# Layer 1 of a two-layer transformer kernel: dispatch tables built in the stage before, keys turned instead of projected twice

## The reference, cut to what matters

```
xn = layernorm(x)                          # 2048 tokens of 256
q, k, v = silu(xn @ Wq), silu(xn @ Wk), silu(xn @ Wv)     # 16 heads of 16
# linear attention in chunks of 128 tokens, per head with decay ld:
scores = (q k^T) * D ;  o = scores v + (q S) * q_decay
S = chunk_decay * S + (k * k_decay)^T v
attn = rmsnorm_per_head(o * sigmoid(xn @ Wg1 @ Wg2)) * norm_w @ Wo
# mixture of experts: 8 experts, 2 for each token, hidden width 512
rw, sel = top_k(softmax(xn @ w_router), 2) ;  rw = rw / sum(rw)
ffn = sum over the 2 chosen e of rw_e * (silu(xn @ w_gate[e]) * (xn @ w_up[e])) @ w_down[e]
out = x + attn + ffn
```

## Time and profile before

| | us |
|---|---|
| median of 3 runs | 1018.13 |
| lowest and highest | 1017.15, 1026.66 |
| the profiled execution's own time | 1027.36 |
| its span, first to last instruction | 1025.4 |
| PE busy in the span | 863.5 (84%) |
| DVE busy | 576.3 (56%) |
| ACT busy | 407.2 (40%) |
| POOL busy | 312.3 (30%) |
| data moved by DMA | 130.52 MB, mean 127 GB/s |

### The profile page before, as it was taken

How to read it: one execution, slowest core, us unless ns; L and a number is a source line. 1 busy time by engine, 2 the same in 40 slices (tenths; PEclk the granted TensorE clock), 3 DMA queues, 4 the chain that set the end, 5 groups by cost and what they waited for, 6 DMA issues and landing times. The chain is left out here.

```text
span 1025.4 us, 14999 instructions
## 1 busy us (share of the span) xinstructions
PE 863.5 (84%) x4608; PEld 501.9 (49%) x4608; DVE 576.3 (56%) x1269; ACT 407.2 (40%) x686; POOL 312.3 (30%) x250
## 2 busy tenths in 40 slices
...
GB/s 270 127 58 143 200 196 186 117 212 54 104 72 55 125 110 127 73 108 109 135 81 75 93 33 156 224 264 271 148 91 104 103 115 94 88 93 89 73 174 143
DMA packets 158625, 130.52 MB, mean 127 GB/s; under 512 B 64144, under 2 KB 140192, under 8 KB 158560
## 3 DMA queue, kind: packets, MB, share of 16 engines
...
...
## 5 line engine op out<-in xcount | busy, mean ns | idle before, releaser
L1291 DVE TENSOR_REDUCE b_negmax<-b_psM 128x1 f32<-128x512 f32 x256 | 162.9, 683 | 59.0 <-PE b_psM L1453 56.3
L1222 ACT ACTIVATE b_probs<-b_psE 128x512 f32<-128x512 f32 x256 | 138.9, 594 | 117.2 <-PE b_psE L1471 116.4
L1453 PE MATMUL b_psM<-b_kst,b_qst 96*128 96x512 bf16 x256 | 99.1, 429 | 34.3 <-DVE b_negmax L1291 17.7
L1471 PE MATMUL b_psE<-b_qst,b_kst 98*128 98x512 bf16 x256 | 89.1, 409 | 15.2 <-ACT b_probs L1222 11.1
...
L1990 PE MATMUL d_psG<-d_w,d_xT 128*128 x156 | 76.8, 615 | 3.0 <-issue 2.1
L1480 PE MATMUL b_psV<-b_probs,b_vst 128*32 128x512 f32 x512 | 74.8, 658 | 2.8 <-ACT b_probs L1222 2.8
L1822 POOL TENSOR_TENSOR d_rs<-d_ss,d_neghalf 128x16 f32<-128x16 f32 x16 | 47.0, 2938 | 98.9 <-DVE d_ss L1918 98.9
L1998 PE MATMUL d_psU<-d_w,d_xT 128*128 x156 | 74.9, 603 | 0.0
L2015 PE MATMUL d_psY<-d_w,d_hidden 128*128 x312 | 74.8, 382 | 0.0
L1471 PEld LDWEIGHTS b_psE<-b_qst,b_kst 98*128 98x128 bf16 x256 | 20.6, 98 | 106.0 <-ACT b_probs L1222 52.1
L1453 PEld LDWEIGHTS b_psM<-b_kst,b_qst 96*128 96x128 bf16 x256 | 24.2, 99 | 94.2 <-DVE b_negmax L1291 68.1
...
...
## 6 DMA issues: line engine op xcount, KB each, us to landing
...
```

What stands on the lines that cost most here:

```text
L1222: nc.scalar.activation(probs[k % PSLOTS][:, h, :], psE[h % 2][:, :], ACT.Exp, scale=float(HD) ** -0.5).then_inc(scores_used[h % 2], 1)
L1291: nc.vector.tensor_reduce(negmax[i][:, t, h:h + 1], psM[:, h % 2, :], AX_X, ALU.max, negate=True).then_inc(rows_used[h % 2], 1)
L1453: nc.tensor.matmul(psM[:, h % 2, :], qst[g][0:STACK, h, t * P:(t + 1) * P], kst[g][0:STACK, h, :], start=True, stop=True).then_inc(rows_re ...
L1471: nc.tensor.matmul(psE[h % 2][:, :], kst[g][0:STACKM, h, k * P:(k + 1) * P], qst[g][0:STACKM, h, :], start=True, stop=True).then_inc(score ...
```

## The change

1. **Tables move.** `Dispatch` is now built in `middle`. `take`, `put` and `expert` outlive the stage. In the steps of batch 3, DVE gets `prepare` after slot 9, `pick` and `positions` after slot 12, `spread_ids` (inblk, ids) after 13, `spread_rows` (inrow) after 14, `owners` and `tables` after 15; PE gets `rank` after slot 12 and `invert` after 15. The three constants are loaded at the start of `middle`, ahead of the loads of head groups 2 and 3.
2. **Gathers first.** `layer1_main` begins with the four gathers on POOL, and SP loads ident, the weights of expert 0 and then chunk 0. The place of `weights_loaded` is as before. In `main_order` the steps of chunk 0 are no longer in front: all 16 chunks are dealt between the blocks from block 1 on. `outputs` moves from step 6 to step 5, right behind `updates`.
3. **Keys turned.** The second projection of the keys goes, with its silu on ACT. Instead PE transposes the k that slot 12 has made (`turn_k`, 8 transposes, slot 13), and DVE's `decay_k` reads them from PSUM in slot 13. The gate moves from slot 13 to 14 and waits there for `kd_done` (not alone). Wk is loaded once.

```
-            loop(sp, attend, {SLOTS - 8: (store_xn,), SLOTS - 4: (store_q,), SLOTS - 3: (store_gate,), SLOTS - 1: (store,)})
+            loop(sp, attend, {SLOTS - 8: (store_xn,), SLOTS - 4: (store_q,), SLOTS - 2: (store_gate,), SLOTS - 1: (store,)})
...
-                               12: (silu_half(1),), 13: (gate,), 14: (silu_kk,),
-                               15: (silu_v,)})
+                               12: (silu_half(1),), 14: (gate,), 15: (silu_v,)})
...
             def decay_k(n):
-                dve.wait_ge(kk_done, n + 1)
+                dve.wait_ge(k_ps, n + 1)
+                dve.wait_ge(stored, STORES * n)
...
-                               7: (normalise, find_next), 8: (split_xT,), 10: (copy_low, fold_next(0)), 11: (copy_lowT, fold_next(1)),
-                               12: (route_weights, fold_next(2)), 13: (first_part, fold_next(3)), 14: (second_part,),
-                               15: (third_part, decay_k)}, ready)
+                               7: (normalise, find_next), 8: (split_xT,), 9: (prepare,), 10: (copy_low, fold_next(0)), 11: (copy_lowT, fold_next(1)),
+                               12: (route_weights, fold_next(2), place), 13: (first_part, decay_k, fold_next(3), spread_ids),
+                               14: (second_part, spread_rows), 15: (third_part, finish_tables)}, ready)
...
+            def turn_k(n):
+                pe.wait_ge(half_done, 2 * n + 2)
+                for t in range(TILES):
+                    for k in range(KT):
+                        at = t % 2 * D + k * P
+                        mm = nc.tensor.transpose(psX[:, t // 2, at:at + P], half[:, k, t * P:(t + 1) * P], ident[:, :])
+                mm.then_inc(k_ps, 1)
...
-                              8: (turn_x,), 9: (project_half(0),), 10: (logits_low,), 11: (turn_low,), 12: (project_half(1),),
-                              13: (project_gate,), 14: (project_tokens(0, gate_done, kk_ps),),
-                              15: (project_tokens(1, kk_done, v_ps),)}, ready)
+                              8: (turn_x,), 9: (project_half(0),), 10: (logits_low,), 11: (turn_low,), 12: (project_half(1), rank),
+                              13: (turn_k,), 14: (project_gate,), 15: (project_v, invert)}, ready)
...
-    order = [("rank", 0, 0)]
-    order += [("light", *step) for step in steps[:7]]
-    order.append(("invert", 0, 0))
-    order += [("light", *step) for step in steps[7:first]]
-    rest = steps[first:]
-    order += [("turn", 0, 0), ("turn", 1, 0), ("gate", 0, 0), ("up", 0, 0), ("turn", 2, 0)]
-    slots, used, given = BLOCKS * 5, 0, 0
+    order = [("turn", 0, 0), ("turn", 1, 0), ("gate", 0, 0), ("up", 0, 0), ("turn", 2, 0)]
+    slots, used, given = (BLOCKS - 1) * 5, 0, 0
...
-            dispatch.load(sp, io)
+            sp.dma_start(ident[:, :], io["ident"]).then_inc(ident_in, 16)
+            load_weights(0)
             load_chunk(0)
...
-            load_weights(0)
             load_weights(1)
             load_chunk(1)
             for e in range(2, E, 2):
                 load_weights(e)
                 load_weights(e + 1)
                 weights_loaded(e - 2)
                 weights_loaded(e - 1)
                 load_chunk(e // 2 + 1)
...
                 elif s == 5:
                     updates(n)
-                elif s == 6:
                     outputs(n)
```

157 lines of the change are left out of this document (85 added, 72 removed).

## The result

The changed kernel is slower by 0.74%: in 20 runs each, beside one another, the median is 1028.37 us (1022.68 to 1034.75) against 1022.85 us (1016.13 to 1032.89), and the ratio is 1.0074 with a 95% interval of 1.005 to 1.0098 (the quotient of the two medians alone is 1.0054, so differences of 0.2% between ratios say little). A second measurement gave 1.0081 (1.0048 to 1.0114). I had forecast a ratio of 0.998 and a time of 1016 us in a range of 1006 to 1027 us. The profiled execution of the changed kernel took 1029.67 us, its span is 1027.9 us.

What follows compares the result with a forecast made beforehand. PE bounds the expert stretch; engine-to-engine chains bound the two stretches ahead. Terms -7.7 + 5.0 + 5.3 + 0 - 3.5 - 1.1 = -2.0 us, from the median 1018.13 to 1016 us, range 1006 to 1027.

Steps and rivals of the forecast that it cites:

- Part 1: Start of the last stage: first gate 30.7 us after the barrier instead of 38.4, -7.7 us (-13.2 to -5.6).
- third rival: Last stage: `load_chunk(2)`, held behind chunk 0, releases experts 2 and 3 late; some 1040 us; chance 0.05.
- Part 2: Expert stretch: chunk 0's 66 matmul records now fall where PE is busy, +5.0 us (0 to +7).
- hand-offs are a little tighter: Expert stretch: steps stand at 0.92 of the places between expert matmuls, not 0.83; no size of its own.
- Part 3: End of `middle`, batch 3 alone: v's store goes out behind k's third part, +5.3 us (+4 to +6.5).
- v starts at about the same time as before, since it needs the gate's PSUM: End of `middle`, batch 3 alone: v is ready at about 631 to 632 us as before.
- The block by POOL: Batch 3 alone: POOL's subtraction holds DVE's inblk, two SBUF operands, adding 0.9 us; `decay_k`, one PSUM operand, is not blocked.
- Part 4: Attention with steps beside it: looped batches 0 us (-3 to +5 for both), last batch -3.5 us (-5 to -1).
- the gate waits for kd: Looped batches: POOL delays `decay_k`, +6 us for two; gain beside the last batch goes to 0; 1026 us; chance 0.12.
- Part 5: Start of `middle`: POOL's second weight subtraction halves, so its masking of the decay ends earlier, -1.1 us (-1.5 to +1).
- that gap: Whole kernel: profiled execution of 1027.36 us lies 0.9% above the median of 1018.13 us, claimed not to affect the sum.
- the signs by which I wanted to see myself wrong: First gate under 26 us, v's store early, looped slots 13 to 15 over 1 us shorter, or less expert-stretch PE idle.

Runs made afterwards that it cites:

- e_ready: Changed kernel, but SP releases expert 0 right behind the four constants, ahead of the later weights and chunk 1; ratio to before 0.9865.
- e_out6: Changed kernel with `outputs` back at step 6, as before the change; ratio to before 1.009.
- e_front: Changed kernel with chunk 0's twelve steps ahead of the first gate and chunks 1 to 15 dealt from block 0 on; ratio to before 1.0006.
- e_gate5: Changed kernel with DVE's `gate_out` and POOL's power of a chunk at step 5 instead of 6; ratio to before 0.9963.
- e_keys: Kernel before with part 3 of the change alone (keys turned, gate in slot 14 behind kd, Wk loaded once); ratio to before 1.0005.
- e_same: Kernel before, unchanged, profiled a second time; ratio to before 0.9979, profiled execution 1025.48 us.
- e_order: Changed kernel with the gate back in slot 13, transposes in 14, `decay_k` in 14 and `second_part` in 15 of looped batches; ratio to before 1.0047.
- e_late: Changed kernel with `first_part` of k in slot 14 and `second_part` in 15 unless the batch is alone; ratio to before 1.0055.
- e_after2: Changed kernel, unchanged, measured and profiled a second time; ratio to before 1.0081, span 1050.6 us.
- e_same3: Kernel before, unchanged, profiled beside the changed one for the second comparison; span 1035.3 us.
- e_same2: Kernel before, unchanged, profiled a third time, on the chip of the second set; span 1039.2 us.
- e_before_late: Kernel before with `first_part` of k moved to slot 14 and `second_part` to 15 (not alone), nothing else; ratio to before 1.0073.

## Why the prediction was wrong, step by step

**Part 1, the start of the last stage: right.** -7.7 us forecast, -7.7 and -7.8 measured; 30.2 us behind the barrier for 30.7, with 49 DMAs in 30 us and the second chunk's first six in 6.07 us for 7.16. (Of the 7.6 us that I put down to those six, only 4.1 are theirs, 7.16 less six at 0.51; the rest lay in the six behind them and in weight DMAs. The total was right all the same.) PE idled 21.2 us at half clock, ended by SP. e_ready shows that this release, and no data, was late. My third rival, a later release held by chunk 0, did not come: PE waits for SP ahead of the first gate and of no other.

**Part 2, chunk 0 in the expert stretch: the mechanism right, the term mis-sized.** +5.0 (0 to +7) forecast, +9.4 and +13.8 measured, above my upper end. The busy time was well counted (6.2 us for 5.7). What failed is the step "hand-offs are a little tighter", which carried no number. "Moving `outputs` next to `updates` costs nothing" held, for e_out6, which undoes the move, is no shorter (324.9 us); but it missed what the move made possible. I had set the idle time to zero because PE had 9.1 us of it to spare. But that idle was itself hand-offs of a chunk's steps; another chunk and closer steps add to it (+3.7 us) and do not fill it. e_front shows that the cost is that of chunk 0 among the blocks (with the closer steps that it brings; the two were not tried apart), and e_gate5 shows the chain: heads, `gate_out`, POOL's power, d_normed.

**Part 3, the end of the middle stage: about right, by a chain that was half wrong.** +5.3 forecast, +5.5 and +6.7 measured; v's store at 633.95 is where I had it once the 4.6 us of the parts ahead are taken off (638.1 - 4.6 = 633.5). The step "v starts at about the same time as before, since it needs the gate's PSUM" failed: the old gate ran ahead of k's silu, the new one behind the transposes and at half clock (3.78 us), and v came 4 to 7 us later. In the changed kernel it is hidden behind the third part of k, with 2.5 us to spare, so that the number held by luck; but it is why part 3 alone gains nothing at this end (e_keys, +3.7 to e_same and +1.8 to the first profile, against my -2). The base had its share too: in the profile that I read the 48 matmuls of keys and v took 8.7 us, in the three others of that kernel 6.0 at full clock, and the barrier stood 33.8 to 34.0 us behind the split and not 35.9.

The block by POOL came as priced. inblk, with two operands in SBUF, took 2.50 us beside POOL's subtraction (621.45 to 623.57) and ended 1.35 us behind it, where the same operation took 1.49 us in the earlier trace rows without POOL; `decay_k`, one operand in PSUM, took its 1.22 us beside the same POOL instruction, unblocked. There `decay_k` had begun 0.16 us ahead of POOL; in the second looped batch of e_order POOL was first, and it was not blocked either:

```profile
480.09 2.12 POOL L1207 TENSOR_TENSOR b_half<-b_half,b_part 128x1024 f32<-128x1024 f32 x1 [15.43 <-PE b_psX L1639]
481.69 1.21 DVE L1402 TENSOR_TENSOR b_kd<-b_psX,b_kdec 128x1024 f32<-128x1024 f32 x1
```

By the Trainium skill (SBUF — State Buffer, "SBUF: two separate sides"), which has the shared pair of ports as an exclusive lock against DVE operations with two SBUF inputs, this is what has to come; the trace agrees, and shows for `decay_k` what no row of before could.

**Part 4, looped batches: wrong.** 0 (-3 to +5) forecast, +3.9 and +2.3 measured, and +6.1 in the slots concerned. The step that failed: "Taking ACT's silu and two table loads and 16 of 24 PE instructions from slots 13 and 14 therefore lets ACT and PE arrive earlier at the same DVE". They do arrive earlier, but the gate then waits for kd, which is queued behind that very wait of DVE. This is my rival "the gate waits for kd", and its price (3 us a batch) is what the slots show, for another reason than the one it named: not POOL's lock on `decay_k`, which is not blocked, but `first_part` ahead of it. The rival's other half, that the gain beside the last batch goes, did not come in the first set (-5.0 us, more than my -3.5) and did in the second (-0.6). e_order and e_late each take this loss out of the slots, by the place of the gate and by the place of `first_part`. The ratio fell with them by 0.34% and 0.26%, less than the 9 us of the slots, so how much of the whole loss this is stays open.

**Part 5:** -1.1 forecast; slots 0 and 1 of the first batch, from 235.5 to 249.1 us before, are 2.6 us shorter (1.0 and 2.3 in e_after2 against e_same3 and e_same2), about what was forecast or more. The whole stretch ahead of the first split is 2.8 and 0.9 us shorter.

**The base.** "nothing in the sum depends on that gap, so I take it from the median": that median was of three runs, and 20 gave 1022.85. Of the 12.4 us between 1016 and 1028.37, 4.7 are this; moved up by them, my range would have been 1011 to 1032 us and held the result, but the direction would have been as wrong as it is. The rest is parts 2 and 4: chunk 0 and the looped batches cost 8.3 and 11.1 us more than forecast in the two sets; in the first, the last batch and the stretch ahead of the first split gave 3.2 us of it back.

Both wrong terms had a bound or a rival near the truth (+7 for chunk 0, +6 for the gate). With the upper ends of parts 2 and 4 my sum is +5.0, 1028 us from the median of 20 runs; I had treated these two ends as unlikely together, and nothing in the profile said so. None of the signs by which I wanted to see myself wrong came: I had watched for slots 13 to 15 to shrink and for PE's idle time to fall, and both grew.

**What stays open.** Why the expert stretch with chunk 0 in it is 4 us longer in the second set, while that of the kernel before is not. In it e_after2 has 2.3 us more idle that no engine releases, ahead of the matmuls of the state, and PE is busy 2.2 us more (307.4 for 305.2). Why e_before_late is slower. And in which stretch the kernel before has its scatter of 19 us: the profiles show it in the middle stage, but none fell on the fastest runs.
